# Order of the score matmuls in the self-attention of a decoder layer: pair the two products for the maxima, then the two transposed ones

## The reference

```python
scores = jnp.einsum('bghnd,bhsd->bghns', q, k)
attn = jax.nn.softmax(scores / SCALE, axis=-1)
out = jnp.einsum('bghns,bhsd->bghnd', attn, v)
```

## Time and profile before

| | us |
|---|---|
| median of 3 runs | 1672.32 |
| profiled execution | 1672.14 |
| its span | 1670.4 |
| `phase_qkv`, to the first A matmul | 0 to 71.2 |
| A matmuls alone | 71.2 to 102.3 |
| the 16 groups | 102.3 to 741.7 |
| cross-attention and experts, from 741.7 with the projection of self-attention | to 1670.4 |

### The profile page before, as it was taken

How to read it: one execution, slowest core, us unless ns; L and a number is a source line. 1 busy time by engine, 2 the same in 40 slices (tenths; PEclk the granted TensorE clock), 3 DMA queues, 4 the chain that set the end, 5 groups by cost and what they waited for, 6 DMA issues and landing times. The chain is left out here.

```text
span 1670.4 us, 34792 instructions
## 1 busy us (share of the span) xinstructions
PE 1625.8 (97%) x12150; PEld 1077.1 (64%) x12150; DVE 1362.2 (82%) x2673; ACT 1092.6 (65%) x2278; POOL 508.0 (30%) x568
## 2 busy tenths in 40 slices
PE   7899999999999999999989999998999999999999
PEld 3443333333333333348579999997898888888887
DVE  6699999999999999927568888886887666666664
ACT  5338888888888888882468888885335454545452
POOL 2000000000000000014036677753553555555550
PEclk9869999999999999999999999999999999999999
DMA  6601211111111111003311313114635333333336
GB/s 219 206 7 38 38 36 31 34 33 33 31 31 32 31 32 31 3 20 101 122 44 38 105 52 120 47 51 151 229 101 144 57 52 58 51 53 57 52 58 174
DMA packets 85192, 116.96 MB, mean 70 GB/s; under 512 B 19051, under 2 KB 64415, under 8 KB 84415
## 3 DMA queue, kind: packets, MB, share of 16 engines
q1 hardware_dynamic: 67248, 90.95, 19.5%
q0 software_dynamic: 13728, 18.88, 7.0%
q10 hardware_dynamic: 4047, 4.91, 1.0%
HBM read 71.25 MB, written 46.60 MB: 71 GB/s over the span
## 5 line engine op out<-in xcount | busy, mean ns | idle before, releaser
L506 DVE TENSOR_REDUCE half_max<-psA 128x1 f32<-128x512 f32 x1024 | 630.3, 683 | 6.6 <-PE psA L559 4.5
L538 ACT ACTIVATE PT<-psB 128x1024 f32<-128x1024 f32 x512 | 520.8, 1026 | 140.2 <-PE psB L569 139.8
L559 PE MATMUL psA<-KS,QS 48*128 48x512 f32 x1024 | 397.6, 470 | 7.9 <-PEq L104 2.0
L569 PE MATMUL psB<-QS,KS 50*128 50x512 f32 x1024 | 377.7, 457 | 0.1
L588 PE MATMUL psO<-PT,VG 128*32 128x256 f32 x4096 | 321.0, 392 | 0.1
L559 PEld LDWEIGHTS psA<-KS,QS 48*128 48x128 f32 x1024 | 163.2, 191 | 232.7 <-DVE half_max L506 174.5
L588 PEld LDWEIGHTS psO<-PT,VG 128*32 128x32 f32 x4096 | 84.6, 108 | 176.5 <-issue 102.9
L475 POOL CAST max_parts<-neg_max 128x16 fp32r<-128x16 f32 x32 | 6.3, 198 | 618.5 <-DVE neg_max L516 618.5
L1515 ACT ACTIVATE x_probs<-x_scores,x_neg_max 128x77 f32<-128x77 f32 x512 | 176.0, 358 | 1.2 <-DVE x_neg_max L1455 1.2
L2283 ACT ACTIVATE swd_high<-WD 128x1024 fp32r x71 | 75.3, 1061 | 150.0 <-PE m_psY L2026 150.0
L1912 POOL DMA_INDIRECT acc<-m_y,tokens x71 | 123.2, 1735 | 145.8 <-DVE m_y L2215 80.3
(11 more groups left out here) (261 smaller groups left out, 2772.5 us busy)
## 6 DMA issues: line engine op xcount, KB each, us to landing
QS<-q_parts SPq DMA_DIRECT2D x96, 128.0 KB
q_parts<-part SPq DMA_DIRECT2D x16, 512.0 KB, 4.3
mx_kept<-cx_mx SPq DMA_DIRECT2D x8, 616.0 KB, 4.9
cx_mx<-mx_kept SPq DMA_DIRECT2D x4, 1232.0 KB, 7.5
KS<-k_parts SPq DMA_DIRECT2D x32, 128.0 KB
xf_rows<-XF SPq DMA_DIRECT2D x32, 128.0 KB, 1.7
acc<-X SPq DMA_DIRECT2D x32, 128.0 KB, 1.8
xf_turned<-n_xfT SPq DMA_DIRECT2D x32, 128.0 KB, 1.8
```

What stands on the lines that cost most here:

```text
L506: dve.tensor_reduce(half_max[:, h * (TB // 2) + t % (TB // 2), n:n + 1], psA[:, bank_of(slot, 2 * v + r), :], axis=AX.X, op=ALU.max).then_ ...
L538: act.activation(PT[:, k % 4, 2 * a:2 * a + 2, :].rearrange("p h n -> p (h n)"), psB[:, u % 2, :, :].rearrange("p a n -> p (a n)"), ACT.Ex ...
L559: pe.matmul(psA[:, bank_of(slot, m), :], QS[top:top + KQ, slot, h // 2, t * P:(t + 1) * P], KS[top:top + KQ, slot, n * HALF:(n + 1) * HALF ...
L569: mm = pe.matmul(psB[:, u % 2, r, :], KS[top:top + KM, slot, c * P:(c + 1) * P], QS[top:top + KM, slot, a, half * HALF:(half + 1) * HALF], ...
```

## The change

The two A matmuls of a unit are issued first, half 0 and then half 1, and after them the two B matmuls, half 0 and then half 1. Before, the order was A0, B1, A1, B0. The same matmuls run on the same data, and each keeps its half, its bank and its semaphores; the wait for `exp_done` stands on the first B matmul as before, which is now the one of half 0.

```diff
-                    for r in range(2):
-                        if has_a:
-                            pass_a(i + ahead, (slot + ahead) % SLOTS, (u + NC + LEAD) % NU, r)
-                        pass_b(i, slot, u, 1 - r, r == 0)
+                    if has_a:
+                        for r in range(2):
+                            pass_a(i + ahead, (slot + ahead) % SLOTS, (u + NC + LEAD) % NU, r)
+                    for r in range(2):
+                        pass_b(i, slot, u, r, r == 0)
```

## The result

The changed kernel took 1690.49 us as the median of four runs (1689.75 to 1696.02), the kernel before 1671.93 in the same comparison: a ratio of 1.0107, with a 95% interval of 1.0079 to 1.0136. That is 18.6 us slower; the interval reaches from 13 to 23 us.

What follows compares the result with a forecast made beforehand. TensorE's own sequence was taken as the bound, with VectorE close behind. Ordinary units 7.8, double units 6.5 and the transpose 2.4 made 16.7 us on 1672.1: 1689 us, range 1683 to 1696, chance 0.70.

Steps and rivals of the forecast that it cites:

- The bound: Self-attention units: TensorE's own sequence sets the 1.24 us unit; VectorE follows closely, at 1.196 alone.
- Ordinary units: Units with one lot of value matmuls: A1 released 0.04 late, average cost 0.02 a unit, 7.8 us in all.
- the transpose: Once in each half group it pushes back the reduces: lateness 0.12 in place of 0.04, 2.4 us in all.
- the 0.05 of the release: From a reduce's end to the A load waiting for it: 0.05 us, read from two places in the rows.
- The double unit: u = 5 and 21, two lots of value matmuls: both B matmuls behind A1 cost 0.24, 27 times, 6.5 us.
- the new start of the ring: Group 3 and like places: the first A matmul's wait for the last reduce at u = 6 swallows 0.24.
- The sum: Whole kernel: 7.8 + 6.5 + 2.4 = 16.7 us slower, giving 1689 us.
- miss its place: Rival, ordinary units: A1's late load put off to the next start of loads; 1702.5 us, chance 0.12.
- alternating halves: Rival, ordinary units: second loads start at once, not 0.11 behind the first; faster, 1664 us, chance 0.05.
- The Trainium skill's rule: Weight loads on TensorE: overlap only across row groups, so the new order would help; the trace disagreed.
- 0.07 us of room: Before the change, A1 in the second pair needs 406.56 and may load from 406.49: 0.07 to spare.

Runs made afterwards that it cites:

- e1: Changed kernel, but units u = 5 and 21, with two lots of value matmuls, keep the old order A0, B1, A1, B0: 1684.7 us, ratio to before 1.0080.
- e5: Changed order with reduces that read only 256 of a tile's 512 columns: 1660.0 us.
- e10: Changed order with reduces of 64 columns only, maxima over an eighth of the keys: 1648.2 us.
- e2: Order of before everywhere, the new order only in units u = 5 and 21: 1680.3 us, ratio to before 1.0057.
- e6: Kernel before, with a ring of two banks in place of three: 1797.9 us.
- e7: Changed kernel, with a ring of two banks in place of three: 1881.3 us.
- e11: Kernel before, reordered to A0, B1, B0, A1, so that B0 too goes ahead of A1: 1672.5 us, ratio 1.0002.
- e3: Changed kernel, with the B pair issued first and the A pair second: 1687.8 us, ratio 1.0115.
- e8: Changed kernel, with the last 20 of the 52 A matmuls before the first group issued twice: 1697.3 us.

## Why the prediction was right

*The bound.* That TensorE's own sequence sets the unit, with VectorE close behind, held: the reduces did not change, and their idle time grew with the units.

*Ordinary units and the transpose.* Forecast 7.8 + 2.4 us for 30 half groups, 0.34 for each. e1, which holds these two alone, shows 9.1 us over 28 half groups, 0.33. The shape was forecast too: in most units the lateness alternates between nothing and 0.04 to 0.05, and the unit between 1.24 and 1.28. That A1's wait for the reduce is the cause is shown by e5 and e10, where it is shorter and ordinary units are back at TensorE's 1.24 with A1 beside A0.

That the sum came out so well is in part luck, as the units of the changed kernel show one by one (means over groups 1 to 14 but 3, 7 and 11). Behind the transpose (u = 12 and 28) A1 is 0.05 to 0.06 late and the unit pays 0.05, not the 0.02 and 0.08 of the forecast; eleven others pay 0.016 each, not 0.02. But u = 7 and u = 23, forecast at 0.02 like any other, pay 0.10: A1 is 0.11 late and they last 1.34. VectorE's and the A loads' rows at u = 6 and 7 of group 5:

```profile
327.10 0.19 DVE L516 TENSOR_REDUCE neg_max<-half_max 128x16 f32<-128x32 f32 x1
327.59 0.69 DVE L506 TENSOR_REDUCE half_max<-psA 128x1 f32<-128x512 f32 x1 [0.31 <-PE psA L559]
...
326.99 0.19 PEld L559 LDWEIGHTS psA<-KS,QS 48*128 48x128 f32 x2 [0.41 <-issue]
...
328.22 0.29 PEld L559 LDWEIGHTS psA<-KS,QS 48*128 48x128 f32 x2 [0.41 <-issue]
```

The reduce of A0 starts 0.60 behind A0's load here, not 0.54 as in the earlier trace rows, and ends at 328.28; A1's load begins at 328.33 (0.29 less its 0.18 behind 328.22). It is the first reduce of scores behind the small one to `neg_max`; why it starts 0.06 later stays open. This place before the change stands in the earlier trace rows: from A0 at 132.32 to the reduce at 132.92 it is 0.60, and from A0 to the release at 133.66 it is 1.34, not 1.28, so 0.10 could have been forecast for this unit. The prediction took only the 0.05 of the release from these rows, and as A1's own place, 0.11 behind A0's, is 133.66 too, they do not show a waiting load by themselves.

*The double unit.* Forecast 0.24 in 27 places, 6.5 us. The profile shows 0.24 (2.31 against 2.07), and e2 5.7 us in the 25 places of groups 1 to 14 that are not hidden by the new start of the ring, 0.23 for each. Group 3 paid 0.92 where a plain group paid 1.08, which is the forecast hiding in part. That both B matmuls stand behind A1 is what costs, as e6 and e7 show in the same stretch of 0.43 against 0.67 and e11 by leaving the price at nothing with B1 ahead. In e3 no B matmul stands behind A1 and the two units still pay 0.23, but there A0 itself comes later.

*The sum.* 16.7 us forecast; 15.0 in groups 1 to 14, and with group 0's share of about 1.1 some 16. The medians differ by 18.6; the 2.5 us beyond are inside their interval, and I cannot say how much of them is the clock in group 0.

*The rivals.* A late load does not miss its place: in the ordinary unit shown A1's load began 0.03 behind A0's, not 0.11, and ordinary units stayed under 1.30 but for u = 7 and 23, where A1's load, 0.11 behind A0's, followed its reduce by the usual 0.05. Loads did not come earlier by alternating halves: the second pair still starts 0.11 behind the first (405.42 against 405.31). The Trainium skill's rule that the prediction weighed (TensorE: Matmul & The Clock Gate, section Part 3: Packing small matmuls), that loads overlap with running matmuls only when the row group differs, does not fit the trace of the new order either. There B0's load starts at 405.42, while A0's matmul, in the same half, runs from 405.31 for some 0.50 by its row.

## What to carry to other kernels

In a queue that runs in order, the place of a wait is a cost of its own: put work that is ready between two instructions that wait for the same slow consumer, even if the pairing in the array looks the same. Before reordering, work out for each waiting instruction when its release comes against when its turn comes; here 0.07 us of room became 0.04 of lateness, and a change without a single added instruction cost 1.1%. Look at the odd iterations apart (skipped work, doubled work, a small extra instruction in the consumer's queue, a new start of a ring): two of 32 units carried over a third of the loss.

## What the runs showed of the hardware

- Two matmuls in different row halves of the array do not keep strictly to the order of the program. In the kernel before, B0's matmul, issued fourth, is recorded as starting ahead of A1's, issued third, in 417 of 486 units, by 3 ns on the median; in the unit of the earlier trace rows its load is ahead as well.
- The half clock can last while TensorE's rows, whose ends are modelled, show no gap: 30.8 us in group 0 of the changed kernel, and from 84.0 to 118.4 us in e8.
- From the end of a reduce's row to the weight load that it releases it is about 0.05 us, at the half clock (98.59 to 98.64) and at the full one (406.54 to 406.59 and 328.28 to 328.33 in the changed kernel).
- A float32 value matmul leaves two rows: the kernel issues four in a unit, and the profile counts eight. The eight value matmuls of a unit that the text ahead of the prediction speaks of are these rows.
